# Rings of six raw units and six halves in place of eight and four, and three moves in the order of work

## The reference

```python
x = x + tanh(g_xattn[0]) * wkv(w, u, layernorm(x), ctx)        # recurrence over time
x = x + tanh(g_ffn[0])   * dense(layernorm(x), W1, W2, W3)     # silu(x W1') * (x W3'), Hadamard, W2'
x = x + tanh(g_xattn[1]) * wkv(decay, first, layernorm(x), ctx)
x = x + tanh(g_ffn[1])   * experts(layernorm(x), gate, w1, w2, w3)   # top 2 of 8 experts
```

## Time and profile before

| | us |
|---|---|
| median of 3 runs | 1458.16 (1457.93 to 1459.09) |
| the profiled execution | 1461.85 |
| its span | 1460.2 |
| dense chunks | 109 to 727 |
| last branch and routing | 727 to 831 |
| expert stage | 831 to the end |

### The profile page before, as it was taken

The page is one execution under the profiler, slowest core; times in us unless marked ns, Lnnn a source line. Parts: engine busy times, 40 slices in busy tenths (PEclk is TensorE's granted clock), DMA queues, the critical chain, the costliest instruction groups (busy, mean ns, idle before and its releaser), DMA issues. The chain is left out here.

```text
span 1460.2 us, 18544 instructions
## 1 busy us (share of the span) xinstructions
PE 1229.2 (84%) x5737; PEld 580.6 (40%) x5738; DVE 725.2 (50%) x1173; ACT 472.9 (32%) x616; POOL 220.8 (15%) x238
## 2 busy tenths in 40 slices
PE   1278897998999879989813299999999999999995
PEld 0034343443554434534413044444444444444442
DVE  7866877968778669687674121222122121212211
ACT  2335556465554553555431011111111111111110
POOL 0000000000000210002020512232232222232232
PEclk9999999999999999999955599999999999999998
DMA  6033396685744977557776287897969897944343
GB/s 256 29 115 102 115 317 202 206 284 159 268 151 140 271 110 260 186 163 215 204 168 231 65 176 171 135 196 138 185 162 195 147 186 150 196 87 93 72 75 56
DMA packets 241020, 242.29 MB, mean 166 GB/s; under 512 B 149840, under 2 KB 154192, under 8 KB 237840
## 3 DMA queue, kind: packets, MB, share of 16 engines
q1 hardware_dynamic: 97632, 167.72, 37.7%
q10 hardware_dynamic: 130368, 51.65, 20.4%
q0 software_dynamic: 12960, 22.15, 7.9%
HBM read 138.68 MB, written 69.65 MB: 143 GB/s over the span
## 5 line engine op out<-in xcount | busy, mean ns | idle before, releaser
L1135 PE MATMUL PS<-weights,xs 128*128 x1872 | 412.8, 381 | 29.4 <-DMA xs<-X 29.4
L1058 PE MATMUL PS<-xs,weights 128*128 128x512 f16 x1536 | 358.1, 391 | 46.2 <-ACT sg L603 31.9
L1135 PEld LDWEIGHTS PS<-weights,xs 128*128 128x128 f16 x1872 | 183.7, 98 | 252.2 <-issue 33.0
L1058 PEld LDWEIGHTS PS<-xs,weights 128*128 128x128 f16 x1536 | 152.3, 101 | 241.7 <-ACT sg L603 33.3
L961 DVE SCALAR_TENSOR_TENSOR A<-A,PS 128x1024 f32<-128x1024 f32 x39 | 47.6, 1222 | 344.9 <-PE PS L1135 320.9
L1070 PE MATMUL PS<-weights,hs 128*128 128x512 f16 x768 | 176.7, 380 | 0.0
L652 ACT ACTIVATE A<-PS 128x1024 f32<-128x1024 f32 x39 | 39.9, 1023 | 313.0 <-PE PS L1135 214.9
L972 DVE TENSOR_SCALAR V<-PS,outl 128x512 f32<-128x512 f32 x39 | 29.3, 752 | 167.5 <-PE PS L1149 149.5
L1070 PEld LDWEIGHTS PS<-weights,hs 128*128 128x128 f16 x768 | 75.2, 98 | 85.7 <-issue 0.8
L400 POOL TENSOR_SCALAR rt<-mv 128x4 f32<-128x4 f32 x16 | 3.7, 229 | 690.0 <-DVE mv L706 690.0
L1149 PE MATMUL PS<-weights,SQ 128*128 x480 | 106.7, 379 | 0.5 <-issue 0.5
(11 more groups left out here) (147 smaller groups left out, 1120.5 us busy)
## 6 DMA issues: line engine op xcount, KB each, us to landing
e<-halves SPq DMA_DIRECT2D x192, 256.0 KB
weights<-e SPq DMA_DIRECT2D x96, 512.0 KB
raw<-ew SPq DMA_DIRECT2D x112, 256.0 KB
X<-ew SPq DMA_DIRECT2D x80, 256.0 KB, 4.3
V<-ctx_cm ACTq DMA_DIRECT2D x7, 1024.0 KB, 6.2
X<-w ACTq DMA_DIRECT2D x4, 1024.0 KB, 5.4
out<-X ACTq DMA_DIRECT2D x4, 1024.0 KB
xn_rows<-SQ ACTq DMA_DIRECT2D x8, 512.0 KB, 5.6
```

The source lines that it names most:

```text
L1058: ins = te.matmul(bank(bk), wj[:, j, w, a, c * P:(c + 1) * P], xs[:, g % 2, b, c, :], start=(k == 0 and c == 0), stop=(k == 2 and c == C - 1))
L1135: ins = te.matmul(bank(n), xTt[k][:, b, c, :], weights_of(off, 2 * I // NT * c + n, a), start=(c == 0 and m == 0), stop=(c == C - 1 and m ...
```

## The change

Five things are done.

1. The ring of four stays, for raw places and halves, and each group that lends X now gives two raw places and two halves (`MORE = 2`; a half of 2 x 512 f16 fills as many bytes as a raw unit). A unit's half has the place of its raw: `pairs[k]` beside `raws[k]`, and each place has its own `unit_out`. So six raw places and six halves are in use where eight and four were, and four and four elsewhere. A high half waits for the store of the unit that last used its place. Before group 3's rows are loaded, SP waits for the last stores from the lent places; POOL does so before its gathers.
2. `UNITS` changes: by chunk (before to after) 3: 1 to 0, 4: 0 to 3, 10 and 11: 4 to 2, 13: 1 to 2, 14: 3 to 4; 20 and 21: 4 to 2, 23: 1 to 2, 24: 3 to 4, 29: 2 to 3, 31: 3 to 4; 32 and 33: 1 to 2, 34: 3 to 4, 39: 4 to 1, 40 and 41: 4 to 2, 43: 1 to 2, 44: 3 to 4; 53: 1 to 2, 54: 3 to 4.
3. `ln` goes from place 2 to place 1: ahead of the Copy.
4. `gate2` and `ranked` of group 0 go from chunk 41 to chunk 40.
5. The weight quarters go from ahead of the Silu (ACT) and of the product (DVE) to after place 2 (ACT, ahead of the further units) and after the further units (DVE).

```diff
-UNITS = [[3, 2, 2, 1, 0, 1, 3, 3, 3, 4, 4, 4, 4, 1, 3, 4],
-         [3, 4, 4, 4, 4, 4, 4, 1, 3, 4, 4, 3, 3, 2, 3, 3],
-         [1, 1, 3, 4, 0, 4, 4, 4, 4, 4, 4, 1, 3, 4, 4, 4],
-         [0, 2, 4, 4, 4, 1, 3, 4, 0, 4, 4, 2, 4, 4, 4, 4]]
+UNITS = [[3, 2, 2, 0, 3, 1, 3, 3, 3, 4, 2, 2, 4, 2, 4, 4],
+         [3, 4, 4, 4, 2, 2, 4, 2, 4, 4, 4, 3, 3, 3, 3, 4],
+         [2, 2, 4, 4, 0, 4, 4, 1, 2, 2, 4, 2, 4, 4, 4, 4],
+         [0, 2, 4, 4, 4, 2, 4, 4, 0, 4, 4, 2, 4, 4, 4, 4]]
-... ("ln", 4, 2) ...
+... ("ln", 4, 1) ...
-GATES = {0: (31, 37, 38, 41, 41), ...
+GATES = {0: (31, 37, 38, 40, 40), ...
+MORE = 2
...
-raws = [ring] + [X[:, 3, i, :] for i in range(TILES)] + [X[:, 0, i, :] for i in range(TILES)]
+raws = [ring] + [X[:, g, i, :] for g in (3, 0) for i in range(MORE)]
+pairs = ([halves[:, k, :, :] for k in range(RING)] +
+         [X[:, g, MORE + i, :].bitcast(F16).rearrange("p (s n) -> p s n", s=2) for g in (3, 0) for i in range(MORE)])
 def unit_high(u):                                   # ACT
+    if PLACES[u][:2] == (RING, 0):
+        act.wait_ge(s["w_lo"], NW)
+    if PLACES[u][:2] == (RING + MORE, 0):
+        act.wait_ge(s["x3_out"], 16)
     act.wait_ge(unit_in[PLACES[u][0]], 16 * (PLACES[u][1] + 1))
-    if u >= RING:
-        act.wait_ge(unit_out[u % RING], 16 * (u // RING))
+    if PLACES[u][1]:
+        act.wait_ge(unit_out[PLACES[u][0]], 16 * PLACES[u][1])
 # SP, at the last unit in a place lent by group 3
     if u == lent:
+        for k in range(RING, RING + MORE):
+            sp.wait_ge(unit_out[k], 16 * USES[k])
         sp.dma_start(xg(3), x_tm[3, :, :]).then_inc(x_in[3], 16)
 # ACT and DVE, chunk(g, j)
-    if n in LATE:                      # ahead of the Silu, ahead of the product
-        w_high(LATE[n])                # w_low(LATE[n])
...
+    if n in LATE:                      # ACT: after place 2; DVE: after the further units
+        w_high(LATE[n])                # w_low(LATE[n])
```

More of the change, by code:

```diff
@@ L1 @@
+import collections
 import itertools
@@ L120 @@
 LEND, LENT, GIVEN = max(LATE), 26, 30
+MORE = 2
 def unit_places():
     done = list(itertools.accumulate(n for row in UNITS for n in row))
-    last = [-1] * RING + [done[LEND] - 1] * 4 + [done[GIVEN] - 1] * 4
-    uses, places = [0] * (RING + 8), []
+    last = [-1] * RING + [done[LEND] - 1] * MORE + [done[GIVEN] - 1] * MORE
+    uses, places = [0] * (RING + 2 * MORE), []
     for u in range(NU):
-        open_ = [k for k in range(RING + 8) if last[k] < u - 1 or k < RING]
+        open_ = [k for k in range(RING + 2 * MORE) if last[k] < u - 1 or k < RING]
         if u >= done[LENT]:
-            open_ = [k for k in open_ if not RING <= k < RING + 4]
+            open_ = [k for k in open_ if not RING <= k < RING + MORE]
         k = min(open_, key=lambda k: (last[k], k))
@@ L138 @@
 PLACES = unit_places()
+USES = collections.Counter(k for k, _, _ in PLACES)
 def bank_fills():
@@ L241, in build @@
         wl = [sem(f"expert_in{n}") for n in range(QUEUES)]
-        unit_in = [sem(f"unit_in{n}") for n in range(RING + 8)]
-        unit_out = [sem(f"unit_out{n}") for n in range(RING)]
+        unit_in = [sem(f"unit_in{n}") for n in range(RING + 2 * MORE)]
+        unit_out = [sem(f"unit_out{n}") for n in range(RING + 2 * MORE)]
         idx_s = [sem(f"idx_in{n}") for n in range(AHEAD)]
@@ L275, in build @@
         four = lambda t: t.rearrange("p (j d) -> p j d", d=D)
-        raws = [raw[:, k, :] for k in range(RING)] + [X[:, 3, i, :] for i in range(TILES)] + [X[:, 0, i, :] for i in range(TILES)]
+        raws = [raw[:, k, :] for k in range(RING)] + [X[:, g, i, :] for g in (3, 0) for i in range(MORE)]
+        pairs = ([halves[:, k, :, :] for k in range(RING)] +
+                 [X[:, g, MORE + i, :].bitcast(F16).rearrange("p (s n) -> p s n", s=2) for g in (3, 0) for i in range(MORE)])
         blockv = ctx.enter_context(nc.Block())
@@ L324, in load_units @@
                             sp.wait_ge(s["w_lo"], NW)
-                        if k == RING + 4 and use == 0:
+                        if k == RING + MORE and use == 0:
                             sp.wait_ge(s["x3_out"], 16)
@@ L347, in _ @@
             due = {chunk_units(*divmod(FIRST["pre", g] + 11, J))[0]: g for g in range(1, NG)}
-            lent = max(u for u, (k, _, _) in enumerate(PLACES) if RING <= k < RING + 4)
+            lent = max(u for u, (k, _, _) in enumerate(PLACES) if RING <= k < RING + MORE)
             for u in range(NU):
                 sp.wait_ge(s["unit_lo"], u + 1)
-                sp.dma_start(e16[u * P:(u + 1) * P, :], halves[:, u % RING, :, :].rearrange("p s n -> p (s n)")).then_inc(unit_out[u % RING], 16)
+                sp.dma_start(e16[u * P:(u + 1) * P, :].rearrange("p (s n) -> p s n", s=2), pairs[PLACES[u][0]]).then_inc(unit_out[PLACES[u][0]], 16)
                 if u in due:
@@ L355, in _ @@
                 if u == lent:
+                    for k in range(RING, RING + MORE):
+                        sp.wait_ge(unit_out[k], 16 * USES[k])
                     sp.dma_start(xg(3), x_tm[3, :, :]).then_inc(x_in[3], 16)
-            for k in range(RING):
-                sp.wait_ge(unit_out[k], 16 * (NU // RING))
+            for k in range(RING + 2 * MORE):
+                sp.wait_ge(unit_out[k], 16 * USES[k])
             sp.wait_ge(s["down_done"], NG * J)
@@ L423, in _ @@
             gp.wait_ge(s["x3_out"], 16 * NG)
+            for k in range(RING + MORE, RING + 2 * MORE):
+                gp.wait_ge(unit_out[k], 16 * USES[k])
             def first_row(i):
@@ L878, in unit_low @@
                 ve.wait_ge(s["unit_hi"], u + 1)
[L879 removed]
+                ve.scalar_tensor_tensor(pairs[PLACES[u][0]][:, 1, :], raws[PLACES[u][0]], SW, pairs[PLACES[u][0]][:, 0, :], MUL, SUB).then_inc(s["unit_lo"], 1)
             def chunk(g, j):
```

10 lines of the change are left out of this document (5 added, 5 removed).

## The result

The changed kernel took 1453.55 us against 1459.88 before (medians of 20 runs each); the ratio is 0.9951, 95% interval 0.9939 to 0.9964. So it gained about 7.1 us by the ratio (6.3 between the medians); 14.4 were forecast. The profiled execution took 1452.16 us, its span 1450.5. The last matmul of the 64 chunks ends at 719.3 us in this trace and at 726.8 in that of before, 7.5 us earlier: the gain lies in the stage that was argued about, with half of its forecast size. (Where a text gives a time for the end of the chunks, 722.0 and 729.5 for these two, it means a point 2.7 us behind that matmul, in every trace alike.)

A forecast was written before the change was run, and what follows sets the result against it. PE's idle time in the dense chunks was priced through DVE, next in line everywhere. Terms +5.0 - 5.2 - 5.4 + 1.0 + 1.7 + 0.7 - 1.2 - 11.0 = -14.4 gave a median of 1443.8 us, range 1437 to 1450, chance 0.52.

The forecast's parts named there:

- the -11.0 for gate, scatter and six halves: Chunks 40 to 45: gate steps and scatter earlier, no store waits with six halves; 11 us gained, between 13.8 and 9.
- Rival 1: Transposes land late, about 515 us, and chunk 41's scans wait ten us; 11 becomes 4, giving 1451; chance 0.16.
- rival 3: Transposes beside the scatter pay per packet, 43 us; chunk 42's product 35 us late, giving 1484; chance 0.07.
- the three signs of being wrong: Chunk 41's scans wait over 5 us for transposes; raw-place waits beyond 5 us; quarters' DVE waits stay at 2.4.
- The round-robin rule: Engines alternate queues packet by packet, so the scatter would barely slow others and 13.8 us come; the prediction did not adopt it.
- Quarters: Chunks 1 to 8: DVE waits for units ahead of its moved weight quarters; +5.0 us, chunk 8 starts at 194.9.
- Rival 2: DVE's idle time in the first chunks takes up the quarters' new waits, so they cost nothing: 1438.8; chance 0.12.
- Chunks 10 to 17 and 20 to 27: Store waits vanish with six halves and DVE has fewer units there: -5.2 and -5.4 us.
- The lent places: SP waits at chunk 26 for a store from the last lent place, with later transfers queued behind: +1.0 us.
- Chunks 32 to 38: One more unit in each of chunks 31 to 34 costs DVE time: +1.7 us at the end of that branch.
- Chunks 53 on: One more unit each in chunks 53 and 54, +0.7 us; store waits of chunks 59 to 62 vanish, -1.2.
- The logarithm: Ln ahead of the Copy: ACT's chain sheds 1.4 us, but DVE's next product starts where it did; 0 on the path.

The follow-up runs named there:

- c_scatter_end: The changed kernel with the scatters of groups 0 and 1 moved behind the chunks: 1438.87 us, ratio 0.9825.
- a_gate41: The changed kernel with gate 0's last two steps back in chunk 41: 1442.28 us, ratio 0.9856.
- a_ln_place2: The changed kernel with the logarithm back at place 2, behind the Copy: 1470.86 us, ratio 1.0036.
- f_list_and_ln: The kernel before with only the new unit list and the logarithm ahead of the Copy: 1443.93 us, ratio 0.9862.
- g_best_pool_load: As d_end_quarters, but POOL, not SP, waits for the last stores from the lent places and loads group 3's rows: 1431.77 us, ratio 0.9773.
- b_gate40: The kernel before with only gate 0's last two steps moved to chunk 40: 1470.99 us, one run, 1.0047 of the median before.
- d_end_quarters: The changed kernel with the scatters of groups 0 and 1 behind the chunks and the weight quarters in their old place: 1434.14 us, ratio 0.9789.

## Why the prediction came out as it did

**What failed: the -11.0 for gate, scatter and six halves.** It measured -3.7 from chunk 38 to 48. I had put the landing of the transposes between no slowing (13.8) and a slowing by 3.3 (9), "since the row lists and the other slow packets all touch DRAM and the transposes go SBUF to SBUF". So 2.8 us were priced for the scatter beside the transposes. With the scatter out of the window (c_scatter_end) the step is -16.2, so it costs 12.4. The clause fell: a transfer that touches no DRAM lands 3.5 to 6 times later beside the scatter (11.8 to 20.0 us for 3.4). Rival 1 is what happened, scans of chunk 41 waiting some ten us (12.45), the term 4 in place of 11, chance 0.16. The sum with its 4 is -7.4, against -7.5 in the traces; that it fits so closely is luck, since the other terms were off by up to 3.4 us each and cancel. The loss per packet of rival 3 did not come: DVE was freed at 512.8, before its 522.

The overlap was misplaced as well. The working had the scatter freed at about 494.4 us and six tenths of the transposes' packets behind 498.6, with the others through at full pace. In the trace DVE frees the scatter at 484.3 us (of the 10.1 us between, 4.4 are what chunk 38 was early), 4.9 us before the first of the transposes is issued, for the gate's steps run ahead of the normalisation (L792, at 484.31) whose result is transposed. So no part of them had the queue to itself: even the first, issued at 489.2, took 11.8 us.

Two of the three signs of being wrong came: the scans' wait (12.45 us, over 5) and the waits for raw loads (9.9 us, over 5).

What the view had shown is the queue's time for a packet, 265 ns for 80, and that it holds for one kind of packet. With no row for another kind beside the scatter, the end with the measured ratio (9) was already the favourable one.

The working also gave 4.7 us to the gate's early steps. a_gate41 shows 1.12 of this wait left without the move, with the new list and rings in place: two edits had been priced for one and the same wait.

**The round-robin rule.** The Trainium skill (DMA: Bandwidth & Descriptors, "Queues, rings and completion order") has an engine take a packet of one queue, then one of the next. I had drawn from it that the scatter's few packets would leave the other queue its pace. The runs disagree with that: 13.0 us for a store beside it, 4.1 beside gathers of as many packets.

**Quarters: +5.0, measured +4.7.** Chunk 8's matmuls start at 194.56 us, 194.9 forecast. Their own undo gives back 4.9 at chunk 8 and 18. Rival 2 is refuted.

**Chunks 10 to 17 and 20 to 27: -5.2 and -5.4, measured -7.0 and -6.9.** The store waits vanished as forecast (32.5 us to 0). PE's busy time shrank too, from 68.65 to 66.57 us and from 68.23 to 66.41 with as many matmuls: 3.9 us of clock, for which the walk with fixed durations had no term. That is about the 3.3 that it missed. The clock and the logarithm can't be told apart here: with the late logarithm (a_ln_place2) the two steps are -5.0 and -4.9 us and the clock is 0.98, with the early one -7.0 and -6.9 and 1.00. Nor do the rings carry most of these steps: with the list and the early logarithm alone (f_list_and_ln) they are -5.0 and -6.0, with ACT still waiting for stores.

**The lent places: +1.0, measured +3.1.** Raw waits of some 6 us stand in this stretch, as foreseen, but g_best_pool_load takes most of them away and chunk 32 doesn't move. So SP's wait isn't the cause; the step from chunk 28 to 32 is 1.2 (a_gate41) to 3.1 us with the rings and 0.9 without them (f_list_and_ln). The kernel before and b_gate40, alike up to chunk 39, differ by 1.7 us in the same step, so much of this is no more than the spread of single traces, and what sets the rest is left open.

**Chunks 32 to 38: +1.7, measured +1.7. Chunks 53 on: +0.7 and -1.2, measured -1.6 and +2.2.** The end went the other way. The store waits there vanished, but the second scatter slows raw loads, and six places ahead are too few for that: "nothing, while the queue runs at its normal pace" carried its own exception, and I gave the exception no price. With both scatters behind the chunks the last chunks lose nothing (-27.3 at chunk 59, -31.6 at 63 in d_end_quarters).

**The logarithm: 0, measured about -12 us by the ratios** inside the changed kernel (-21 at the end of the chunks, in a trace that overstates it), -9.9 with the new list alone. The term was priced at nothing by the chunk's old units, and that failed too. Whether the walk of the new list already held part of this gain in its other terms isn't on record; if it didn't, the other terms promised that much too much, and the sum came as near as it did by luck. Without this edit the changed kernel is slower than before.

## What to carry to other kernels

Before a transfer is moved or a stage is advanced, look at what the queues carry in the new window, and if a small-row write to DRAM is among it, price every transfer beside it at three to six times its usual landing, as here, SBUF to SBUF ones too; better, issue that write where little waits (behind the chunks it still cost some 4 us). Price edits together when they stand in front of the same wait: here list and rings had already taken 3.6 of the 4.7 us that the gate's move was meant to bring, and the logarithm's place was priced at nothing by the old list and is worth 10 to 12 us in the new one. A stall that goes can bring more than its idle time, because the clock stays up: 11 of 22 us here.

## What the runs showed of the hardware

Indirect writes of 8-byte rows to DRAM, eight in a scatter and 1.0% of the engines' time in their own queue from 489 to 513 us, when six of them are issued, slow all other transfers for some 20 us: stores of 256 KB land in 13.0 us, transposes in 11.8 to 20.0 us; beside the second scatter raw loads take 15.7 us. Eight gathers through like indices, 2.3% of the time, leave them at 4.1 to 4.5 us. TensorE's granted clock was 0.90 from 480 to 530 us with a stall of 8.77 us in that window, 10.2 us of it at 1.2 GHz, and 1.00 (2.4 GHz) without the stall.
